# A macaron block (FFN, causal linear attention, FFN) in fp32: another order of the instructions on all four engines

## The reference, cut to what matters

```
x = x + 0.5 * ffn(layernorm(x))
x = x + attn(layernorm(x), w_attn, w_proj)
x = x + 0.5 * ffn(layernorm(x))            # x: 16 x 1024 x 512, fp32

def attn(x, w_attn, w_proj):               # 16 heads of 32
    q, k, v = split(x @ w_attn)
    q, k = elu(q) + 1, elu(k) + 1
    # causal, along the 1024 tokens of a sequence
    y_t = (q_t . sum_{s<=t} k_s v_s^T) / (q_t . sum_{s<=t} k_s + 1e-6)
    return y @ w_proj

def ffn(x):                                # 64 channels, 16 hidden units in each
    s = x @ Win + bin_
    g = sum_h relu(s * W1[:, h] + b1[:, h]) * W2[:, h] + b2
    return g @ Wout + bout
```

## Time and profile before

| | |
|---|---|
| median of 3 runs | 2392.15 us (2391.70 to 2393.62) |
| the profiled execution | 2391.91 us, span of the trace 2390.1 us |
| PE busy | 2294.7 us (96%), 32450 matmuls |
| DVE busy | 1940.2 us (81%) |
| ACT busy | 1426.8 us (60%) |
| POOL busy | 812.3 us (34%) |
| DMA | 111.51 MB, 47 GB/s |

### The profile page before, as it was taken

One profiled execution on the slowest core, in us unless ns is written; L12 is line 12 of the kernel. 1 busy time (PEld: TensorE's weight loads), 2 busy tenths in 40 slices (PEclk: granted clock), 3 DMA queues, 4 the chain that ended last, 5 costly groups with the idle time before them and its releaser, 6 DMA issues.

```text
span 2390.1 us, 74560 instructions
## 1 busy us (share of the span) xinstructions
PE 2294.7 (96%) x32450; PEld 1763.3 (74%) x32450; DVE 1940.2 (81%) x3346; ACT 1426.8 (60%) x2267; POOL 812.3 (34%) x864
## 2 busy tenths in 40 slices
PE   3999999999999999999999999999999999999995
PEld 3777777777777777777777777777777777777773
DVE  6678888888888888888888988888988888887766
ACT  5555656555656555656655656655656655656654
POOL 5233233333333333333333333333333333333311
PEclk7999999999999999999999999999999999999997
DMA  5001102111101111111111111111111111110110
GB/s 172 20 20 37 55 20 56 55 55 37 55 20 56 55 55 38 55 34 42 55 55 40 52 38 38 55 55 44 48 38 38 56 55 49 43 38 20 37 38 36
DMA packets 49592, 111.51 MB, mean 47 GB/s; under 512 B 8177, under 2 KB 10225, under 8 KB 45170
## 3 DMA queue, kind: packets, MB, share of 16 engines
q1 hardware_dynamic: 49266, 106.74, 15.3%
HBM read 72.12 MB, written 34.60 MB: 45 GB/s over the span
## 4 chain that ended last, share of the span: by engine, by line
PE 74%; DVE 15%; issue 4%; POOL 4%; ACT 1%; SPq 1%; DMA 0%; DVEq 0%; POOLq 0%; ACTq 0%
PE bank L993 33%; PE att L993 13%; PE att L1011 6%; PE att L1085 5%; PE att L1110 5%; DVE st L664 3%; DVE res L714 3%; DVE acc_psum L702 2%; PE att L1101 2%; PE bank L1036 2%; PE bank L1073 2%; POOL z L358 2%; PE att L1027 2%; PE bank L1121 1%; DVE xf L692 1%
## 5 line engine op out<-in xcount | busy, mean ns | idle before, releaser
L449 ACT ACTIVATE xhat<-res,nmr,rstd 128x512 f32<-128x512 f32 x384 | 302.2, 808 | 353.8 <-DVE nmr L672 291.0
L464 ACT ACTIVATE ffr<-ffs,b1c,w1c 128x512 f32<-128x512 f32 (+1 forms) x544 | 427.9, 812 | 20.5 <-DVE acc_psum L702 13.9
L702 DVE SCALAR_TENSOR_TENSOR acc_psum<-ffr,w2c,acc_psum 128x512 f32<-128x512 f32 (+1 forms) x510 | 382.6, 750 | 48.8 <-ACT ffr L464 27.6
L362 POOL TENSOR_SCALAR_AFFINE_SELECT A<-A 128x512 f32<-128x512 f32 x256 | 157.0, 638 | 705.0 <-ACT A L426 705.0
L350 POOL TENSOR_TENSOR res<-res,hbout 128x512 f32<-128x512 f32 x256 | 352.2, 1393 | 4.0 <-ACT xhat L449 3.4
L664 DVE BATCH_NORM_STATS2 st<-res 128x6 f32<-128x512 f32 x384 | 260.7, 679 | 16.7 <-DMA res<-in_L_attn_x_dram 11.0
L358 POOL TENSOR_TENSOR z<-qT,z 128x512 f32<-128x512 f32 x128 | 165.9, 1296 | 268.6 <-DVE zc L744 118.3
L993 PE MATMUL att<-xh,wa_h 128*128 128x512 f32 x584 | 235.2, 403 | 1.9 <-DVE xl L681 1.9
L993 PE MATMUL att<-xh,wa_l 128*128 128x512 f32 x584 | 231.3, 396 | 0.0
L993 PE MATMUL att<-xl,wa_h 128*128 128x512 f32 x584 | 231.2, 396 | 0.0
L993 PE MATMUL bank<-wa_h,xh 128*128 128x512 f32 x504 | 214.7, 426 | 0.5 <-issue 0.5
(11 more groups left out here) (128 smaller groups left out, 4967.2 us busy)
## 6 DMA issues: line engine op xcount, KB each, us to landing
res<-in_L_attn_x_dram SPq DMA_DIRECT2D x32, 1024.0 KB, 5.3
xf<-scratch SPq DMA_DIRECT2D x128, 256.0 KB, 4.4
out_dram<-res SPq DMA_DIRECT2D x32, 1024.0 KB, 4.7
scratch<-rden SPq DMA_DIRECT2D x128, 8.0 KB, 1.5
kT<-in_L_attn_w_attn_dram SPq DMA_DIRECT2D x1, 1024.0 KB, 5.3
qT<-in_L_attn_w_attn_dram SPq DMA_DIRECT2D x1, 1024.0 KB, 10.9
v<-in_L_attn_w_attn_dram SPq DMA_DIRECT2D x1, 1024.0 KB, 14.2
A<-in_L_attn_w_proj_dram SPq DMA_DIRECT2D x4, 256.0 KB, 14.0
```

The lines of the kernel that those rows point to most:

```text
L362: eng.affine_select(out=A[:, h, :, :], in_=A[:, h, :, :], compare_op=ALU.is_ge, fill=0.0, base=0, pattern=[[0, 4], [1, P]], channel_multip ...
L449: eng.activation(xhat[t % 2][:, :], res[b % SLOTS][:, t, :], ACT.Identity, bias=nmr[:, n, b % 2, t:t + 1], scale=rstd[:, n, b % 2, t:t + 1 ...
L464: eng.activation(ffr[i % 2][p, :], ffs[p, :], ACT.Relu, bias=b1c[p, i:i + 1], scale=w1c[p, i:i + 1]).then_inc(s_hr, 1)
L702: eng.scalar_tensor_tensor(psum[p, :], r[p, :], w2c[p, i:i + 1], psum[p, :], ALU.mult, ALU.add).then_inc(s_hm, 1)
```

## The change

It reorders the calls of all four engines' lists and the list of banks. No instruction is added or taken out, and no shape, buffer or semaphore is changed. Counted as above, a full block has 15 stretches before and 12 after. Before: [den 0, 1], [key 0], [den 2, 3, ff_in 0], [ff_in 1], [scores 0], [attend 0, update 0, key 1], [channels 0, scores 1], [attend 1, update 1], [key 2, scores 2], [attend 2, update 2], [channels 1, scores 3], [attend 3, channels 2], [channels 3], [ff_out 0, key 3], [update 3, ff_out 1 to 3]. After: [den 0, 1], [den 2, 3], [ff_in 0, key 0, ff_in 1], [scores 0, key 1], [attend 0, update 0], [scores 1, channels 0], [attend 1, update 1], [key 2, scores 2, channels 1], [attend 2, update 2], [channels 2, scores 3], [attend 3, key 3, channels 3], [update 3, ff_out 0 to 3].

PE:

```diff
 
             for j in range(NB + 2):
                 if on(j):
+                    project(j, 0, 0)
                     project(j, 1, 0)
                     project(j, 1, 1)
-                    project(j, 0, 0)
+                    project(j, 1, 2)
                     project(j, 0, 1)
-                    project(j, 1, 2)
+                    project(j, 0, 2)
                     project(j, 1, 3)
-                    project(j, 0, 2)
                     den(j, 0)
                     den(j, 1)
                     project(j, 0, 3)
                     values(j, 0, 0)
-                    key(j, 0)
                     values(j, 0, 1)
+                    values(j, 1, 0)
                     den(j, 2)
                     den(j, 3)
+                    values(j, 1, 1)
                 if on(j - 1) or on(j + 2):
                     ff_in(j, 0)
                 if on(j):
-                    values(j, 1, 0)
+                    key(j, 0)
                 if on(j - 1) or on(j + 2):
                     ff_in(j, 1)
                 if on(j):
-                    values(j, 1, 1)
+                    values(j, 2, 0)
                     scores(j, 0)
-                    values(j, 2, 0)
+                    key(j, 1)
                     values(j, 2, 1)
                     attend(j, 0)
                     update(j, 0)
-                    key(j, 1)
                     values(j, 3, 0)
                     values(j, 3, 1)
+                    scores(j, 1)
                 if on(j + 1):
                     channels(j + 1, 0)
                 if on(j):
-                    scores(j, 1)
                     outer(j, 0, 0)
                     attend(j, 1)
                     update(j, 1)
                     outer(j, 0, 1)
                     key(j, 2)
                     scores(j, 2)
+                if on(j + 1):
+                    channels(j + 1, 1)
+                if on(j):
                     outer(j, 1, 0)
                     attend(j, 2)
                     update(j, 2)
                     outer(j, 1, 1)
                 if on(j + 1):
-                    channels(j + 1, 1)
+                    channels(j + 1, 2)
                 if on(j):
                     scores(j, 3)
                     outer(j, 2, 0)
                     attend(j, 3)
-                if on(j + 1):
-                    channels(j + 1, 2)
-                if on(j):
-                    outer(j, 2, 1)
-                if on(j + 1):
-                    channels(j + 1, 3)
-                if on(j):
-                    outer(j, 3, 0)
-                if on(j - 1) or on(j + 2):
-                    ff_out(j, 0)
                 if on(j) and updates(j, 3):
                     key(j, 3)
-                if on(j):
+                if on(j + 1):
+                    channels(j + 1, 3)
+                if on(j):
+                    outer(j, 2, 1)
+                    outer(j, 3, 0)
                     outer(j, 3, 1)
                 if on(j) and updates(j, 3):
                     update(j, 3)
                 if on(j - 1) or on(j + 2):
+                    ff_out(j, 0)
                     ff_out(j, 1)
                     ff_out(j, 2)
                     ff_out(j, 3)
```

The list of banks:

```diff
         for j in range(NB + 2):
-            give(ATT + RING, ("k", j, 0), ("k", j, 1), ("q", j, 0), ("q", j, 1), ("k", j, 2), ("k", j, 3), ("q", j, 2),
-                 ("den", j, 0), ("q", j, 3), ("v", j, 0), ("key", j, 0))
+            give(ATT + RING, ("q", j, 0), ("k", j, 0), ("k", j, 1), ("k", j, 2), ("q", j, 1), ("q", j, 2), ("k", j, 3),
+                 ("den", j, 0), ("q", j, 3), ("v", j, 0), ("v", j, 1))
             if on(j - 1) or on(j + 2):
                 give_all("in", j, 0)
-            give(ATT + RING, ("v", j, 1))
+            give(ATT + RING, ("key", j, 0), ("v", j, 2))
             give_all("sc", j, 0)
-            give(RING, ("v", j, 2), ("up", j, 0), ("key", j, 1), ("v", j, 3), ("xT", j + 1, 0))
+            give(RING, ("key", j, 1), ("up", j, 0), ("v", j, 3))
             give_all("sc", j, 1)
-            give(RING, ("y", j, 0), ("up", j, 1), ("key", j, 2))
+            give(RING, ("xT", j + 1, 0), ("y", j, 0), ("up", j, 1), ("key", j, 2))
             give_all("sc", j, 2)
-            give(RING, ("y", j, 1), ("up", j, 2), ("xT", j + 1, 1))
+            give(RING, ("xT", j + 1, 1), ("y", j, 1), ("up", j, 2), ("xT", j + 1, 2))
             give_all("sc", j, 3)
             give(RING, ("y", j, 2))
-            give(ATT + RING, ("xT", j + 1, 2), ("xT", j + 1, 3), ("y", j, 3), ("o0", j - 1, 0), ("o1", j + 2, 0),
-                 ("key", j, 3), ("up", j, 3), ("o0", j - 1, 1), ("o1", j + 2, 1), ("o0", j - 1, 2), ("o1", j + 2, 2),
-                 ("o0", j - 1, 3), ("o1", j + 2, 3))
+            give(ATT + RING, ("key", j, 3), ("xT", j + 1, 3), ("y", j, 3), ("up", j, 3),
+                 ("o0", j - 1, 0), ("o1", j + 2, 0), ("o0", j - 1, 1), ("o1", j + 2, 1),
+                 ("o0", j - 1, 2), ("o1", j + 2, 2), ("o0", j - 1, 3), ("o1", j + 2, 3))
         wa_st = [qT, kT, v]
```

POOL:

```diff
             for j in range(NB + 2):
                 if on(j):
                     zsum(j, 0)
+                    zsum(j, 1)
+                if on(j + 2):
+                    bias(1, j + 2, 0)
+                if on(j):
+                    zsum(j, 2)
+                    zsum(j, 3)
+                if on(j + 2):
+                    bias(1, j + 2, 1)
+                if on(j + 3):
+                    rstds(L1, j + 3)
                 if on(j - 1):
                     bias(0, j - 1, 0)
-                if on(j):
-                    zsum(j, 1)
-                    zsum(j, 2)
-                    zsum(j, 3)
-                if on(j + 2):
-                    bias(1, j + 2, 0)
-                    bias(1, j + 2, 1)
-                    bias(1, j + 2, 2)
                 if on(j):
                     mask(j, 0, 0)
                     mask(j, 0, 2)
                 if on(j - 1):
                     bias(0, j - 1, 1)
                 if on(j):
+                    mask(j, 1, 2)
                     mask(j, 1, 0)
-                    mask(j, 1, 2)
                     mask(j, 2, 0)
                     mask(j, 2, 2)
+                    mask(j, 3, 0)
+                    mask(j, 3, 2)
+                if on(j + 2):
+                    bias(1, j + 2, 2)
                 if on(j - 1):
                     bias(0, j - 1, 2)
+                if on(j):
+                    rstds(L3, j)
+                if on(j - 1):
                     bias(0, j - 1, 3)
-                if on(j):
-                    mask(j, 3, 0)
-                    mask(j, 3, 2)
-                    rstds(L3, j)
-                if on(j + 3):
-                    rstds(L1, j + 3)
                 if on(j + 2):
                     bias(1, j + 2, 3)
                     rstds(L2, j + 2)
```

DVE, the front of a block and its end (in the middle `update`, `ynorm` and `ysplit` of tile 0 come two `hidden` earlier, those of `channels` are moved, and `shift(L1, j + 3)` comes right behind `ysplit(j, 3)`):

```diff
             for j in range(NB + 2):
                 if on(j):
                     project(j, 1, 0)
-                    project(j, 0, 0)
+                    project(j, 1, 1)
                     zsum(j, 0)
-                    project(j, 0, 1)
+                if on(j + 2):
+                    transposed(1, j + 2, 0)
                 if on(j) and carries(j):
                     carry(j, 0)
-                if on(j):
-                    project(j, 1, 1)
+                if on(j + 2):
+                    transposed(1, j + 2, 1)
+                if on(j):
                     zsum(j, 1)
-                    project(j, 1, 2)
+                    project(j, 0, 0)
+                    project(j, 0, 1)
+                if on(j + 3):
+                    stats(L1, j + 3, 0)
                 if on(j) and carries(j):
                     carry(j, 1)
                 if on(j + 2):
-                    transposed(1, j + 2, 0)
-                    transposed(1, j + 2, 1)
-                if on(j):
-                    project(j, 1, 3)
+                    transposed(1, j + 2, 2)
+                if on(j):
+                    project(j, 1, 2)
                     zsum(j, 2)
+                if on(j + 3):
+                    stats(L1, j + 3, 1)
                 if on(j) and carries(j):
                     carry(j, 2)
                 if on(j):
+                    project(j, 1, 3)
+                    project(j, 0, 2)
                     zsum(j, 3)
-                    project(j, 0, 2)
                 if on(j) and carries(j):
                     carry(j, 3)
-                if on(j + 2):
-                    transposed(1, j + 2, 2)
                 if on(j):
                     project(j, 0, 3)
+                if on(j + 2):
+                    transposed(1, j + 2, 3)
                 if on(j + 3):
-                    stats(L1, j + 3, 0)
-                if on(j + 2):
-                    transposed(1, j + 2, 3)
+                    stats(L1, j + 3, 2)
                 if on(j):
                     rec(j)
                 if on(j + 3):
-                    stats(L1, j + 3, 1)
-                    stats(L1, j + 3, 2)
```

(68 more changed lines are left out.)

82 lines of the change are left out of this document (41 added, 41 removed).

## The result

The changed kernel takes 2409.38 us (median of 4 runs, 2404.74 to 2416.82) where the kernel before, beside it, takes 2392.73 (2391.70 to 2393.62). The ratio is 1.0072, with a 95% interval of 1.0058 to 1.0086: slower by 0.7%, where the forecast was 20 us faster and the range ended at 2389. The profiled execution of after took 2416.82 us (span 2415.0), the slowest of its four, so its trace shows 24.9 us over the profiled execution of before, 8 us more of a loss than the medians do.

What follows compares the result with a forecast made beforehand. PE's stream, busy 98.7% of the main loop, was taken to set the time. Edges -14, waits removed -17 and waits made +11 gave -20 us, a forecast of 2371.5 us with a range of 2358 to 2389.

Steps and rivals of the forecast that it cites:

- part 6: SyncE's spread, sums, ff_out's banks, POOL's biases, start and end: slack suffices, no cost; at most 1 us at the ends.
- Parts 1 to 3: PE's edges at ff_out, den with ff_in, and the transpositions: -0.44 us a block, -14 us over 32 blocks.
- (a): outer(j, 3, 0) on PE: less cover, so it waits 0.27 us for DVE's yl in odd blocks, +4 us.
- Part 4: Even blocks: den's wait for POOL's z (-9 us) and ff_in's wait behind den (-8 us) go, together -17 us.
- Part 5: New waits on PE at outer(j, 3, 0), attend(j, 0) and den(2), den(3): +11 us, bounds 0 and 28.
- rival by kinds of product: Every change between kinds of product on PE costs 0.2 us; edges give -6 us, not -14; 2379; chance 0.12.
- (b): attend(j, 0) follows scores(j, 0) sooner and waits about 0.15 us for POOL's masks in even blocks, +2 us.
- (c): den(2), den(3) wait for z 3, put at +27.4 to +28.1: 0.15 us a block, +5 us.
- slack 0.1 for the last ff_out: End of the ff_out run: its bank is read in time, with 0.1 us to spare, so no wait.
- Rival E: load(j + 3) lands late, DVE's stats wait for it and den waits for z: slower, 2419 us; chance 0.13.

Runs made afterwards that it cites:

- experiment 10: Kernel before with only ff_out(j, 0) joined to its sisters and outer(j, 3) ahead of ff_out's additions on DVE: 2390.57 us, ratio 0.9994.
- experiment 4: Kernel after with the spread sent in two halves, tiles 0 and 1 first, nothing left out: 2387.25 us, ratio 0.9981.
- experiment 9: Kernel before with only den's bank taken out of the four of att: 2386.48 us, ratio 0.9974.
- experiment 8: Kernel after with values(j, 1, 1) between the parts of ff_in, the spread in two and den's bank outside att: 2360.80 us, ratio 0.9870.
- experiment 1: Kernel after, ynorm multiplying by a constant tile so it doesn't wait for the spread; transfers stay: 2399.20 us, ratio 1.0030.
- experiment 2: Kernel after, ynorm not waiting for the spread and the four spreading transfers left out too: 2385.88 us, ratio 0.9972.
- 3: Control: kernel before, with ynorm's wait for the spread and the spreading transfers both left out: 2390.17 us, ratio 0.9988.
- 6: Kernel after with values(j, 1, 1) moved back between the two parts of ff_in: 2408.01 us, ratio 1.0065.
- 7: Kernel after with values(j, 1, 1) between the parts of ff_in and the spread in two halves: 2380.44 us, ratio 0.9951.
- 13: Kernel after with 32 small matmuls (128 instructions, half a period) ahead of TensorE's first product: 2408.28 us, ratio 1.0065.
- shift experiments: Small matmuls ahead of TensorE's first product: 64 in after 2427.99 us, in before 2408.13; 32 in after 2408.28, in before 2395.02.

## Why the prediction was wrong

The forecast was -20, the result is +17. Every term of the sum can be read off the trace, and most of them came; what failed is what was costed at nothing, in part 6: a wait for the spread, and PE's own supply of instructions.

**Parts 1 to 3, the edges (-14): right in sum, not shown one by one.** key(j, 0) between the parts of `ff_in` takes 0.58 or 0.59, as taken; den(2), den(3) by themselves take 0.58. The `ff_out` run of even blocks takes 3.10. Its join alone (experiment 10) shortened them by 0.28 of the 0.39 forecast. Blocks in which PE isn't stopped show the sum of parts 1 to 5: blocks 16 and 15 of experiment 4 take 70.47 and 70.69, where I gave 70.7 and "about 70.4", the latter without (a). Against blocks 14 and 15 of the kernel before, and with the waits of parts 4 and 5 and of the last `ff_out` taken out as measured, that is -0.6 a block for the edges, where I gave -0.44 (bounds -0.2 and -0.6). The rival by kinds of product put them at -6 us instead of -14. This sum speaks against it; the time of experiment 10 is nearer to its price. It changed 8 us at most and decided nothing.

**Part 4, the waits of even blocks (-17): right.** No den waits for z, and `ff_in` doesn't wait behind den (taken at 8 us; experiment 9 makes it 6). k 0 on DVE follows this row, at +10.8 in block 17, where I counted +11:

```profile
1303.75 0.17 DVE L674 SCALAR_TENSOR_TENSOR nmr<-mv,rstd 128x4 f32<-128x4 f32 x1 [0.88 <-POOL rstd L330]
```

**Part 5, waits made (+11): half right.** (b) came: the large products ahead of attend(j, 0) take 1.60 to 1.79 in even blocks and 1.57 in odd ones. (a) is in odd blocks only, as said, but the large products around outer(j, 3, 0) take 4.89 for 4.39, so 0.50, not 0.27: the transposition and half product of cover was shorter than I took it. (c), the wait at den(2), den(3), didn't come at all: z 3 ended at +27.15, ahead of the +27.4 to +28.1 that I gave it. The large products between `scores(j, 3)` and `attend(j, 3)` take 1.81 where I counted 1.60, in both parities, even in experiment 8. But in the kernel before it was those between `scores(j, 2)` and `attend(j, 2)` that took 1.81, and they take 1.57 now. So it moved from tile 2 to tile 3 and doesn't change the sum; what makes it I haven't tried.

**Part 6, "Places with nothing": here it failed, three times.**

*SyncE.* The sentence was "spread(j) waits for ff_in, which ends 1.4 later in the block while attend(j, 0) is only 0.4 later; ynorm(j, 0) keeps some 0.4." The distance was right: from the end of `ff_in` to `attend(j, 0)` there are 4.69 us after and 5.69 before. The slack was not. The spread lands 7.4 us behind `ff_in` in the mean of the full blocks, before and after alike (6.6 to 8.4): it isn't slower. `ynorm(j, 0)` on DVE stood 8.3 us behind `ff_in` before. Now it could start at 6.5 to 6.7, as it does in experiment 4 where it has nothing to wait for: PE takes 1.0 off, and my list for DVE, which puts it two `hidden` earlier, the rest. So there is no slack, DVE waits 23 times, 0.8 on average, and `scores(j, 1)` behind it. Taking that wait away gives 10 us (experiment 1). The prediction had the slack without a row for it, and left DVE's own move out.

*What a transfer does to PE.* I asked only when the spread lands for its reader. Its 1 MB also holds up the packet with PE's next instructions: to 3.9 us behind the boundary ahead, where it is 1.3 without the transfers. With the new order PE is at the next boundary 4.9 us on and stops, in all 14 odd blocks. With the transfers taken out as well there are 13 us less (2 against 1), and 2.5 at most of that is there before (3). In two halves nearly all of it is gone with nothing left out (4).

*The joined parts of `ff_in`.* I gave the join no gain, and no loss. Some 260 products in 4.6 us bring two boundaries 2.6 us apart, where values(j, 1, 0) made it 3.45 (one part alone is 128 of them in 2.1 us). It stops PE for 0.38 a block in the mean, some 12 us over the run, by over 0.3 us in 7 of 14 even blocks and 6 of 14 odd ones; values(j, 1, 1) back between them ends it (6 and 7), and shifting the stream moves it (13). The distance alone doesn't decide: block 17 has 2.6 us too, and passes, with its packet at +29.99, while in block 8 it is at +30.78. That 6 gained nothing by itself hides this: it let den's bank wait and the landing back in.

A fourth, small: "slack 0.1 for the last ff_out". It waits 0.28 in odd blocks, 4 us, as experiment 10 shows by itself.

**The sum anew.** Profiled execution against profiled execution: -28 by the blocks (70.47 and 70.69 unstopped, as above, against the means before, 72.04 and 70.84, 16 blocks of each, whose own stops are in them), +36 by stops, +9 by the wait for the landing (experiment 1 is 18.0 below in its profiled execution, 8.8 of it fewer stops). That makes 17 of the 24.9; the other 8 are waits and stops of under 0.3 and what the ends of the run changed, which I didn't itemise.

**Rival E** had the right sign and a time 10 us off (2419), by the wrong mechanism, so that nearness is luck. DVE's stats wait for the load 5 times, 12.6 us in all, where they waited 11.0 before; that isn't it. No rival was about PE's own instructions. The shift experiments show that the mechanism is the supply: the stops keep their count and change their place. The packets show what PE waits for. Why a packet starts late while a spread runs, in a queue or for want of a DMA engine (91% of them are busy there), no run here tells.

## What to carry to other kernels

Price an order of small products by instructions for each us, not only by edges: large products between two dense runs are cover for the supply, and a join that saves an edge of 0.1 to 0.4 us can bring a stop of 0.3 to 2. Where a stall has no semaphore and sits in the middle of a run, number the engine's instructions, look at the count modulo the unit of supply, and at when the last instruction packet started; then put a half period of small instructions ahead of all, which moves such stops and no others. A broadcast of 1 MB has two readers to think of: the one that waits for it, and all that fetches beside it; and a bank list is part of an order, since the same list with den in another bank was worth 20 us more.

## What the runs showed that was not expected

All stops of PE that no semaphore explains fall at one count modulo 256 of its 65,608 instructions, in after and in the variants of it that keep its joined `ff_in`, 36, 30, 23, 23, 31 and 29 times. In after they last 0.3 to 2.3 us, and nearly all end 2.2 to 3.0 us after the start of an instruction packet. A small fp32 matmul (1 row, 32 columns) is four instructions, two of them products, and a row of 32 that write the same bank takes 13.9 us, 0.43 each (experiment 13), so it is no filler for an idle gap. The expectation there put each at 0.215, which is one product. And four runs of the kernel after spread over 12 us, where 27 of the kernel before, beside experiments 1 to 4, keep within 6.2. The number of stops doesn't make this: experiment 13 has 29 of them and keeps within 3.0, and experiment 2, without the transfers, has 23 and keeps within 4.0 in 10 runs. That it comes of when a transfer and a packet meet is a reading that wasn't tried.
